# Earlier loads, another split of small steps, and weight maxima on ScalarE in the first stage of a two-layer cross-attention kernel

## The chip, the cores and the metric

The kernel runs on one core of one Trainium2 chip. The metric is the device time of one execution in microseconds (us), as the median of several runs. The engines are called PE (TensorE), DVE (VectorE), ACT (ScalarE), POOL (GpSimd) and SP (SyncE, which here issues transfers). A line number such as L986 is a line of the kernel before.

## The reference, cut to what matters

There are two layers over `x` of 4 x 1024 rows and 1024 columns. Layer 0 is a cross-attention that is one matrix product, layer 1 a softmax attention, and each is followed by a feed-forward part. The change touches only what must be done before the second half can start: the quantised product of layer 0, and the preparation of the weights of both feed-forward parts.

```python
def quant_dequant_act_1x128(x):            # x, after a layernorm: one scale per row and 128 columns
    amax = max(abs(xb)); safe = maximum(amax, 1e-4)
    return float8_e4m3(xb * (448 / safe)) * (safe / 448)
# the context: the same with one scale per block of 128 x 128
x = x + tanh(g_xattn[0]) * quant(layernorm(x)) @ quant(context).T
# the ternary feed-forward part
scale_x = max(abs(rms_norm(layernorm(x)) * gamma))        # one number over all rows
scale_w = mean(abs(weight)); w_q = round(clip(weight / scale_w, -1, 1))
x = x + tanh(g_ffn[0]) * (quantise8(...) @ w_q.T) * scale_w
# layer 1: softmax attention with the context as keys and values, then 8 experts (Wa, Wb), top 2
```

The one number `scale_x` needs all 32 row tiles of the first product, so the kernel has a stage 1 (this product, and the preparation of weights), then a short reduction, and then a stage 2 with all the rest.

## The kernel before, in words

Rows come in 32 tiles of 128, eight to a batch. Stage 1 is a software pipeline that is written out by hand on each engine as a loop over steps `j` from -11 to 33, and the order of the calls within a step is the order of the instructions on that engine. Engines meet only through semaphores. Step `j` works on several tiles at once.

A **row tile** `n` takes this way: SP loads it (`load_x`). DVE takes mean and variance (`x_stats`, L970 and L976), POOL the reciprocal root (`x_rstd`, L453 and L455), ACT subtracts the mean (`centre`, L620). DVE takes eight block maxima (`x_max`, L1004) and makes of them the scales in three small instructions of 8 columns (L1008, L1010, L1012). POOL makes the factors that undo the scale, as a high and a low part, in five small instructions (`x_factors`, L460 to L468). ACT scales (`x_scale`, L610), DVE prepares the rounding to eight bits in three wide instructions (`x_round_start`: L981 takes the exponent, L984 the step, L986 adds it), POOL subtracts it again (`x_round`, L482). ACT and POOL make the high and low half (`x_high`, L610; `x_low`, L475). SP transposes both, PE multiplies them with the context (L809), DVE adds the product to the row tile (`finish_x1`, L1070 and L1073), ACT squares it (`x1_square`, L653), and DVE takes a weighted maximum (`x1_max`, L1077). In step `j`, DVE does `x_max` of tile `j+3`, `x_stats` of `j+4`, `x1_max` of `j-2`, `x_round_start` of `j+2`, and `finish_x1` of `j-1`.

A **context tile** `m` is loaded by eight transfers of 64 KB (`load_c_rows`, L280). DVE takes its maximum (`c_max`, L1017). When all eight of a batch are in, `c_widest` and `c_factors` make the scales, with a transpose on PE between them (L785). Then ACT scales (L638), DVE prepares the rounding in the same three lines L981, L984 and L986 (`c_round_start`), POOL finishes it (`c_round`, L487), PE spreads it (`fill`, L797) and ACT writes the product's operands (`c_evict`, L647). The steps with `c_factors` are called table steps: -3, 5 and 13. One row of scratch for the rounding step serves the row tiles (XSTEP), another the context (CSTEP), so the next rounding waits until POOL has read the last.

**Weights.** From step 9 on, 24 pieces of the weights are loaded and DVE takes the sum or the maximum of each (`weight_stat`, L1082), two in a step. From step 24 on (`PREP`), eight rounds prepare three pieces each: ACT scales them (L658 to L660), DVE clips and rounds the ternary one (L1120, L1123) and takes the low halves of the others (L1128). The three raw pieces have one buffer each, so a round's loads wait for the round before (`load_prep`).

**The reduction.** When the last square is in, POOL takes two powers over all 32 columns (L531, L533), DVE and PE find the one maximum (L1177 to L1191), and the signal `go` (L1196) opens stage 2, whose first DVE instruction is L1201.

Of the kernel before, what the change touches and what calls it, by code (L numbers as in the profile page):

```python
# [5 lines left out]
P = 128  # L6
# [3 lines left out]
KB = D // P  # L10
# [22 lines left out]
TINY = 1e-30  # L33
# [12 lines left out]
STAT, PREP = 9, 24  # L46
# [4 lines left out]
W_TURN_AFTER = PREP - 3 + C_EVICT  # L51
FILL_HI, FILL_LO = 2.0 ** 6, 2.0 ** 14
# [13 lines left out]
def flamingo_two_layers(nc, x, ctx_in, g_xattn, g_ffn, w0, gamma, router_w, wa, wb, out):  # L66
    x_rows = x.rearrange("b s d -> (b s) d")
    c_rows = ctx_in.rearrange("b s d -> (b s) d")
    c_sets = ctx_in.rearrange("b (s r) (k q) -> b r s k q", s=GROUPS, k=KB)
# [6 lines left out]
    with ExitStack() as stack:  # L76
# [52 lines left out]
        W0, WA_RAW, WB_RAW = slot[11], slot[12], slot[3]  # L129
# [7 lines left out]
        CQ = lo_hi(rings[2][:, 3])  # L137
        w_hi = [wa_hi[:], arena[0][:].rearrange("p (k n) -> p k n", k=KB)]
# [4 lines left out]
        xd, xt1, xt2 = small(KB), small(KB), small(KB)  # L143
# [15 lines left out]
        ea, ec, ejunk, eab = (slot[6][:, i * TILES:(i + 1) * TILES] for i in range(4))  # L159
# [53 lines left out]
        c_in = signals("c_in", C_RING, 16 * CHUNK)  # L213
# [8 lines left out]
        x_d, x_hi, x_lo, x_turned = signal("x_d", 5), signal("x_hi"), signal("x_lo"), signals("x_turned", 2, 32)  # L222
# [39 lines left out]
        def weight_slot(t, kind):  # L262
            return t[:].rearrange("p (e r) -> p e r", e=E) if kind == 1 else t[:]
# [17 lines left out]

        @block.sync
        def _(sp):
            def load_c(m):
                after(sp, c_q, m - C_RING)
                for r in range(CHUNK):
                    load_c_rows(sp, m, r)

            for m in range(0, PER_BATCH, 2):
                load_c(m)  # L290
# [12 lines left out]
            def load_stat(t):  # L303
                kind, r = divmod(t, KB)
                after(sp, st_red, t - 2)
                sp.dma_start(weight_slot(WST[t % 2], kind), weight_tile(kind, r)).then_inc(st_in[t % 2].sem, 16)

            def load_prep(r):
                if r == 0:
                    sp.wait_ge(st_red.sem, st_red.at(3 * KB - 1))  # L310
                    sp.wait_ge(c_q.sem, c_q.at(TILES - 1))
                else:
                    sp.wait_ge(w_lo_set.sem, w_lo_set.at(r - 1))
                    sp.wait_ge(w_tern.sem, w_tern.at(r - 1))
                for kind, t in enumerate((W0, WA_RAW, WB_RAW)):
# [1058 lines left out]
```

## Time and profile before

| | us |
|---|---|
| median of 3 runs (2175.8 to 2178.02) | 2176.89 |
| the profiled execution, its own time | 2178.21 |
| its span, from the first to the last instruction | 2176.4 |
| busy in the span: PE, DVE, ACT, POOL | 1881.9, 1603.7, 1247.6, 909.7 |
| first product added (`finish_x1` of tile 0), last (tile 31) | 120.42, 567.43 |
| first DVE instruction of stage 2 | 585.15 |

The profile is of one execution. Busy is the time in which an engine had an instruction in flight. It includes time in which an instruction that had started was held up, so a busy engine need not be an engine at work: two instructions of the same shape with very different durations are the sign of it. The whole of what follows lies in the first 585 us.

### The profile page before, as it was taken

The numbers are of one execution on the slowest core, as the hardware profiler recorded it, in microseconds if no ns is written. First come the engines' busy times: TensorE is split into PE (matmuls) and PEld (weight loads), VectorE is DVE, ScalarE is ACT, GpSimd is POOL, SyncE is SP. The second block draws the span as 40 slices with busy tenths as digits, with TensorE's granted clock in tenths as the row PEclk, the third lists the DMA queues.
The fourth block names the chain that finished last, engine by engine and source line by source line (L and its number), as shares of the span: only waits on it lengthen the run. The fifth ranks groups of instructions, "written<-read, shape, count | busy, mean of one in ns | idle before, by whom it ended". The sixth has DMA issues, their size and how long they took to land.

```text
span 2176.4 us, 26455 instructions
## 1 busy us (share of the span) xinstructions
PE 1881.9 (86%) x8968; PEld 845.8 (39%) x8968; DVE 1603.7 (74%) x2297; ACT 1247.6 (57%) x2011; POOL 909.7 (42%) x1290
## 2 busy tenths in 40 slices
PE   1398768967548999999999999999999999999997
PEld 0144334423213444444444444444444444444443
DVE  5899989997356777777777777677777777777761
ACT  2677657765145556556565656556655656565650
POOL 2687868763223333333333333333333333333320
PEclk9999889988768999999999999999999999999998
DMA  5465656667447888887888787888888787878781
GB/s 142 137 158 149 196 144 188 165 184 203 131 89 141 167 162 162 159 163 153 169 158 172 159 170 151 160 168 165 157 160 165 153 166 161 170 159 170 129 151 43
DMA packets 924743, 339.97 MB, mean 156 GB/s; under 512 B 850753, under 2 KB 899905, under 8 KB 924609
## 3 DMA queue, kind: packets, MB, share of 16 engines
q1 hardware_dynamic: 920000, 336.19, 72.2%
q10 hardware_dynamic: 4608, 2.10, 0.4%
q8 instruction: 71, 1.16, 0.2%
q14 instruction: 64, 0.52, 0.1%
HBM read 92.83 MB, written 33.55 MB: 58 GB/s over the span
## 4 chain that ended last, share of the span: by engine, by line
DVE 35%; issue 18%; ACT 18%; PE 11%; POOL 9%; DMA 5%; SPq 4%; POOLq 0%; ACTq 0%; DVEq 0%
ACT slot L704 8%; DVE tiny L1227 7%; DVE tiny L970 5%; POOL tiny L567 5%; ACT arena L696 5%; POOL tiny L565 3%; PE sc L809 3%; DMA slot<-slot 3%; SPq L280 3%; DVE slot L1231 3%; ACT tiny L690 2%; DVE arena L1239 2%; DVE slot L1214 2%; DMA probs<-slot 2%; ACT slot L718 2%
## 5 line engine op out<-in xcount | busy, mean ns | idle before, releaser
L1231 DVE SCALAR_TENSOR_TENSOR slot<-arena,tiny,slot 128x1024 f16<-128x1024 f32 x256 | 328.4, 1283 | 313.7 <-ACT slot L704 313.7
L866 PE MATMUL sc<-arena,slot 128*128 128x512 f16 x1536 | 376.9, 386 | 34.6 <-ACT arena L696 24.9
L704 ACT ACTIVATE slot<-arena,tiny 128x1024 f16<-128x1024 f32 x256 | 293.7, 1147 | 178.3 <-POOL tiny L567 164.8
L565 POOL TENSOR_SCALAR tiny<-tiny 128x1 f32<-128x1 f32 x256 | 98.9, 386 | 698.1 <-ACT arena L696 698.1
L1227 DVE TENSOR_REDUCE tiny<-sc 128x1 f32<-128x1024 f32 x256 | 306.3, 1206 | 16.9 <-PE sc L866 16.5
L696 ACT ACTIVATE arena<-sc,tiny,head_tab 128x1024 f32<-128x1024 f32 x256 | 308.4, 1205 | 8.6
L690 ACT ACTIVATE tiny<-tiny,head_tab 128x1 f32<-128x1 f32 x256 | 73.9, 289 | 353.0 <-DVE tiny L1227 353.0
L809 PE MATMUL sc<-probs,slot 128*128 128x512 f16 x768 | 184.4, 404 | 66.1 <-DMA slot<-slot 65.5
L866 PEld LDWEIGHTS sc<-arena,slot 128*128 128x128 f16 x1536 | 151.2, 99 | 224.0 <-ACT arena L696 30.7
L882 PE MATMUL accs<-probs,arena 128*128 128x512 f16 x512 | 195.0, 381 | 13.8 <-issue 13.5
L849 PE MATMUL accs<-wb_hi,slot 128*128 128x512 f16 x512 | 195.1, 381 | 8.3 <-DMA slot<-slot 8.3
L851 PE MATMUL accs<-wa_hi,slot 128*128 128x512 f16 x512 | 196.8, 384 | 0.0
L850 PE MATMUL accs<-wa_lo,slot 128*128 128x512 f16 x512 | 196.5, 384 | 0.0
L849 PE MATMUL accs<-wa_hi,slot 128*128 128x512 f16 x512 | 196.2, 383 | 0.0
L883 PE MATMUL accs<-probs,arena 128*128 128x512 f16 x512 | 195.2, 381 | 0.0
L884 PE MATMUL accs<-probs,arena 128*128 128x512 f16 x512 | 195.1, 381 | 0.0
L850 PE MATMUL accs<-wb_lo,slot 128*128 128x512 f16 x512 | 195.1, 381 | 0.0
L851 PE MATMUL accs<-wb_hi,slot 128*128 128x512 f16 x512 | 195.0, 381 | 0.0
L567 POOL TENSOR_TENSOR tiny<-tiny,neg_one 128x1 f32<-128x1 f32 x256 | 160.1, 625 | 21.3
L809 PE MATMUL sc<-wa_hi,slot 128*128 128x512 f16 x512 | 139.5, 390 | 25.7 <-DMA slot<-slot 18.0
L809 PEld LDWEIGHTS sc<-probs,slot 128*128 128x128 f16 x768 | 77.7, 103 | 171.0 <-DMA slot<-slot 70.9
L551 POOL TENSOR_TENSOR slot<-slot 128x512 f16<-128x512 f32 x64 | 74.1, 1158 | 146.0 <-ACT slot L733 146.0
(195 smaller groups left out, 3183.2 us busy)
## 6 DMA issues: line engine op xcount, KB each, us to landing
arena<-in_x SPq DMA_DIRECT2D x32, 512.0 KB, 3.5
x_scratch<-arena SPq DMA_DIRECT2D x32, 512.0 KB, 3.0
slot<-x_scratch SPq DMA_DIRECT2D x32, 512.0 KB, 4.0
slot<-in_ctx SPq DMA_DIRECT2D x32, 512.0 KB, 4.3
out<-arena SPq DMA_DIRECT2D x32, 512.0 KB, 3.4
slot<-in_L_ffn_weight SPq DMA_DIRECT2D x16, 512.0 KB, 3.9
slot<-in_L_ffn_Wa SPq DMA_DIRECT2D x16, 512.0 KB, 5.0
slot<-in_L_ffn_Wb SPq DMA_DIRECT2D x16, 512.0 KB, 5.5
```

The costliest lines, as they stand in the source:

```text
L567: pool.tensor_tensor(rinv[c % 2][:], rsum[c % 2][:], neg_one[:], ALU.pow).then_inc(s_ri.sem, 1)
L696: act.activation(PF[c % 2], sc[:, c % 2, :], ACT.Exp, bias=nbias[c % 2][:], scale=head_tab[:, n, 1:2], accum_out=rsum[c % 2][:]).then_inc( ...
L704: act.activation(PH[c % 2], PF[c % 2], ACT.Identity, scale=rinv[c % 2][:]).then_inc(s_ph.sem, 1)
L809: mm = pe.matmul(sc[:, j % 2, h * HALF:(h + 1) * HALF], lhs[:, cols], rhs[:, k, h * HALF:(h + 1) * HALF], start=start, stop=stop)
L849: pe.matmul(accs[:, a, :], lhs_hi, r_hi[:, k, cols], start=k == 0, stop=False)
L850: pe.matmul(accs[:, a, :], lhs_hi, r_lo[:, k, cols], start=False, stop=False)
L851: mm = pe.matmul(accs[:, a, :], lhs_lo, r_hi[:, k, cols], start=False, stop=k == KB - 1)
L866: mm = pe.matmul(sc[:, c % 2, h * HALF:(h + 1) * HALF], q[i][:, c * P:(c + 1) * P], k[j][:, h * HALF:(h + 1) * HALF], start=start, stop=stop)
L883: pe.matmul(accs[:, ACC_V, :], v[0][:, cols], PT[:, h, KB + j, :], start=False, stop=False)
L884: mm = pe.matmul(accs[:, ACC_V, :], v[1][:, cols], PT[:, h, j, :], start=False, stop=j == KB - 1)
L1227: dve.tensor_reduce(nmx[c % 2][:], sc[:, c % 2, :], AX.X, ALU.max, negate=True).then_inc(s_mx.sem, 1)
L1231: dve.scalar_tensor_tensor(out=PL[c % 2], in0=PF[c % 2], scalar=rinv[c % 2][:], in1=PH[c % 2], op0=ALU.mult, op1=ALU.subtract).then_inc(s_ ...
```

## The change

It has these parts.

- **Loads.** The context of the first batch and three tiles more come in three groups (4, 4 and 3 tiles), each as eight transfers over all tiles of the group, one for each block of 128 columns and 16 partitions wide (`load_c_columns`), four from SP and four from ACT. Tiles 11 to 14 come in two pairs in the same way. The first two row tiles are loaded ahead of them, and their whole preparation stands ahead of the loop on all engines, between the context's first maxima.
- **Small steps.** L1008 and L1012 become instructions with two tensor inputs (the constant lies in a small tile of 8 columns). The five instructions of `x_factors` on POOL become three on DVE, two-input ones too, right behind `x_max`.
- **Weight maxima.** `weight_stat` moves from DVE to ACT, as an absolute value or a square with a sum, about one a step from step 0 to 20, and POOL takes two roots afterwards.
- **Weight preparation.** The raw pieces get a second set of buffers, `load_prep` runs up to two rounds ahead, and on ACT `weight_high` stands behind `x1_square`, not ahead of it.
- **Reduction.** POOL's powers are taken four columns at a time from step 24 on, so that the last four are left for the end.
- `round_start` is split into `round_step` and `round_add`, which are called one after the other.

The order on POOL in a step of the kernel before with a row tile and a context tile (`x_rstd`, `x_factors`, `x_round`, `c_round`, `x_low`):

```order
L453 TENSOR_SCALAR tiny<-xmv 128x1 [waits x_st]
L455 TENSOR_TENSOR tiny<-tiny,neg_half 128x1 [waits x_ra]
L460 TENSOR_SCALAR tiny<-xsafe 128x8 [waits x_am]
L462 TENSOR_SCALAR tiny<-tiny 128x8 [waits x_d]
L464 TENSOR_TENSOR tiny<-tiny 128x8 [waits x_d]
L466 TENSOR_TENSOR slot<-tiny 128x8 [waits x_d]
L468 TENSOR_TENSOR slot<-tiny,slot 128x8 [waits x_d]
L482 TENSOR_TENSOR slot<-slot,arena 128x1024 [waits x_u]
L487 TENSOR_TENSOR wb_lo<-wb_lo,slot 128x1024 [waits c_fill,c_u]
L475 TENSOR_TENSOR slot<-slot 128x1024 [waits x_d,x_q]
```

The same step in the changed kernel (L514 and L516 are `x_rstd`, L530 is `x_round`, L535 `c_round`, L523 `x_low`):

```order
L514 TENSOR_SCALAR tiny<-xmv 128x1 [waits x_rs,x_st]
L516 TENSOR_TENSOR tiny<-tiny,neg_half 128x1 [waits x_ra]
L530 TENSOR_TENSOR slot<-slot,arena 128x1024 [waits x_lo,x_hi,x_u]
L535 TENSOR_TENSOR wb_lo<-tern,slot 128x1024 [waits c_fill,c_u]
L523 TENSOR_TENSOR slot<-slot 128x1024 [waits x_turned0,x_d,x_q]
```

The five small instructions are gone, and `x_rstd` stands right ahead of `x_round`.

On DVE, `x_max` and what follows it up to the statistics of the next tile, before:

```order
L1004 TENSOR_REDUCE tiny<-slot 128x8 [waits x_xc]
L1008 TENSOR_SCALAR xsafe<-tiny 128x8 [waits x_rs,x_am]
L1010 RECIPROCAL tiny<-xsafe 128x8 [waits x_am]
L1012 TENSOR_SCALAR xk<-tiny 128x8 [waits x_am]
L970 BN_STATS tiny<-arena 128x6 [waits x_in1]
```

And in the changed kernel:

```order
L1092 TENSOR_REDUCE tiny<-slot 128x8 [waits x_d,x_k,x_xc]
L1096 SCALAR_TENSOR_TENSOR xsafe<-tiny 128x8 [waits x_rs,x_am]
L1099 RECIPROCAL tiny<-xsafe 128x8 [waits x_am]
L1101 SCALAR_TENSOR_TENSOR xk<-tiny 128x8 [waits x_am]
L1107 SCALAR_TENSOR_TENSOR tiny<-xsafe 128x8
L1110 SCALAR_TENSOR_TENSOR slot<-xsafe,tiny 128x8 [waits x_d]
L1113 TENSOR_TENSOR slot<-xsafe,slot 128x8 [waits x_d]
L1051 BN_STATS tiny<-arena 128x6 [waits x_st,x_in1]
```

Five instructions of 8 columns with two tensor inputs and one reciprocal stand there now, where there were two with one input and the reciprocal.

On ACT, a step of the weight preparation before (L610 is `x_high` and then `x_scale`, L620 `centre`, L658 to L660 `weight_high`, L653 `x1_square`):

```order
L610 ACTIVATE slot<-slot 128x128 x8
L610 ACTIVATE slot<-slot,xk 128x128 x8
L620 ACTIVATE slot<-arena,xmv 128x1024
L658 ACTIVATE slot<-slot,tiny 128x1024
L659 ACTIVATE wa_hi<-slot,tiny 128x1024
L660 ACTIVATE wb_hi<-slot,tiny 128x1024
L653 ACTIVATE slot,row_tab<-arena,row_tab 128x1024
```

And in the changed kernel (L714 is `x1_square`, L721 to L723 `weight_high`):

```order
L671 ACTIVATE slot<-slot 128x128 x8
L671 ACTIVATE slot<-slot,xk 128x128 x8
L681 ACTIVATE slot<-arena,xmv 128x1024
L714 ACTIVATE slot,row_tab<-arena,row_tab 128x1024
L721 ACTIVATE slot<-slot,tiny 128x1024
L722 ACTIVATE wa_hi<-slot,tiny 128x1024
L723 ACTIVATE wb_hi<-slot,tiny 128x1024
```

The square, which waits for the step's `finish_x1` on DVE, has moved ahead of the three weight instructions.

The diff, cut to its core:

```diff
+STAT_STEPS = 21
+C_GROUPS = ((0, 4), (4, 4), (8, 3))
+C_PAIRS = {11: 2, 12: 0, 13: 2, 14: 0}
+X_EARLY, NORM_COLS = 2, 4
+PREP_TILES = (25, 26, 27)
...
+        RAW_EARLY = [rings[1][:, 2], rings[1][:, 3], rings[2][:, 2]]
+        RAW_LATE = [XP[tile % X_RING] for tile in PREP_TILES]
+        def raw(kind, r):
+            if r % 2 == 0:
+                return RAW[kind]
+            return (RAW_EARLY if r < KB // 2 else RAW_LATE)[kind]
...
+        def load_c_columns(eng, m, count, k, sig):
+            b, i = divmod(m, PER_BATCH)
+            at = m % C_RING
+            ring = (tern, wb_hi, wb_lo)[at // 4][:].rearrange("p e n -> p (e n)").bitcast(F32)
+            dst = ring[k::KB, (at % 4) * D:(at % 4 + count) * D].rearrange("p (r q) -> p r q", q=P)
+            src = c_columns[b, k][:, i * CHUNK:(i + count) * CHUNK]
+            eng.dma_start(dst, src).then_inc(sig.sem, 16)
...
             def load_prep(r):
-                if r == 0:
+                if r < 2:
...
-                    sp.wait_ge(w_lo_set.sem, w_lo_set.at(r - 1))
-                    sp.wait_ge(w_tern.sem, w_tern.at(r - 1))
+                    sp.wait_ge(w_lo_set.sem, w_lo_set.at(r - 2))
+                    sp.wait_ge(w_tern.sem, w_tern.at(r - 2))
+                if r == KB // 2 + 1:
+                    sp.wait_ge(x1_out.sem, x1_out.at(PREP_TILES[-1]))
+                    sp.wait_ge(e_sq.sem, e_sq.at(PREP_TILES[-1]))
...
+                for r in range(KB):
+                    late = 1 if r % 2 and r > KB // 2 else 2
+                    if j == PREP - late + r:
+                        load_prep(r)
...
-            def x_factors(n):
-                pool.wait_ge(x_am.sem, x_am.at(n, 2))
-                pool.tensor_scalar(xd[:], xsafe[:, n % 2], -AMP / FP8_MAX, 1.0, ALU.mult, ALU.mult).then_inc(x_d.sem, 1)
...
+            def row_norms(first, count):
+                cols = slice(first, first + count)
+                pool.wait_ge(e_sq.sem, e_sq.at(first + count - 1))
+                pool.tensor_scalar(ea[:, cols], row_tab[:, cols, 1], ...)
+                pool.tensor_tensor(ec[:, cols], ea[:, cols], neg_half[:, cols], ALU.pow).then_inc(g_pool.sem, 1)
+                pool.wait_ge(e_max.sem, e_max.at(first + count - 1))
+                pool.tensor_tensor(eab[:, cols], row_ab[:, cols], half_pow[:, cols], ALU.pow).then_inc(g_pool.sem, 1)
...
         @block.scalar
-            for m in range(1, PER_BATCH, 2):
-                for r in range(CHUNK):
-                    load_c_rows(act, m, r)
-            act.wait_ge(const_in.sem, 48)
+            for g, (first, count) in enumerate(C_GROUPS):
+                for k in range(KB // 2, KB):
+                    load_c_columns(act, first, count, k, c0_in[g])
...
+            def weight_stat(t):
+                act.wait_ge(st_in[t % 2].sem, st_in[t % 2].at(t // 2))
+                act.activation(WST[t % 2][:], WST[t % 2][:], ACT.Abs if t < KB else ACT.Square,
+                               accum_out=wst[:, t:t + 1]).then_inc(st_red.sem, 1)
+            for n in range(X_EARLY):
+                centre(n)
+            for n in range(X_EARLY):
+                x_scale(n)
+            for n in range(X_EARLY):
+                x_high(n)
...
+                if is_x(j - 1):
+                    x1_square(j - 1)
+                for t in stats_of(j):
+                    weight_stat(t)
                 if PREP <= j < PREP + KB:
                     weight_high(j - PREP)
-                if is_x(j - 1):
-                    x1_square(j - 1)
...
         @block.vector
-                dve.tensor_scalar(xsafe[:, i], xam[:], xrstd[:, i:i + 1], ACT_EPS, ALU.mult, ALU.max).then_inc(x_am.sem, 1)
+                dve.scalar_tensor_tensor(out=xsafe[:, i], in0=xam[:], scalar=xrstd[:, i:i + 1], in1=eps8, op0=ALU.mult,
+                                         op1=ALU.max).then_inc(x_am.sem, 1)
...
+            def x_factors(n):
+                d, hi, lo = xsafe[:, n % 2], xdh[:, n % 4], xdl[:, n % 4]
+                dve.scalar_tensor_tensor(out=xt2[:], in0=d, scalar=SPLIT7, in1=d, op0=ALU.mult, op1=ALU.subtract)
+                dve.scalar_tensor_tensor(out=hi, in0=d, scalar=SPLIT7, in1=xt2[:], op0=ALU.mult, op1=ALU.subtract)
+                dve.tensor_tensor(lo, d, hi, ALU.subtract).then_inc(x_d.sem, 1)
...
-            for m in range(PER_BATCH):
+            for n in range(X_EARLY):
+                x_stats(n)
+            for n in range(X_EARLY):
+                x_max(n)
+            for m in range(PER_BATCH // 2):
+                c_max(m)
+            for n in range(X_EARLY):
+                x_round_start(n)
+            for m in range(PER_BATCH // 2, PER_BATCH):
                 c_max(m)
...
-                if STAT <= j < STAT + 12:
-                    weight_stat(2 * (j - STAT))
-                    weight_stat(2 * (j - STAT) + 1)
```

## Rows read from the trace of the kernel before

**Rows 1.** Stretches: busy us of each engine and count, granted clock, transfer share, GB/s
```profile
120.42:415.82 295.40, 242.66 (x1131) 112.47 (x1129) 279.41 (x437) 197.94 (x441) 230.32 (x209) 0.93 0.62 170
...
567.43:585.23 17.80, 0.63 (x2) 0.25 (x2) 4.42 (x16) 1.24 (x2) 12.11 (x3) 0.59 0.38 147
```

**Rows 2.** Timeline of DVE, `finish_x1`: start us, duration us, engine, line
```profile
120.42 1.28 DVE L1070 SCALAR_TENSOR_TENSOR arena<-sc,tiny,arena 128x1024 f32<-128x1024 f32 x1
...
161.20 1.28 DVE L1070 SCALAR_TENSOR_TENSOR arena<-sc,tiny,arena 128x1024 f32<-128x1024 f32 x1
...
180.31 1.28 DVE L1070 SCALAR_TENSOR_TENSOR arena<-sc,tiny,arena 128x1024 f32<-128x1024 f32 x1
...
192.09 1.28 DVE L1070 SCALAR_TENSOR_TENSOR arena<-sc,tiny,arena 128x1024 f32<-128x1024 f32 x1
...
275.10 1.28 DVE L1070 SCALAR_TENSOR_TENSOR arena<-sc,tiny,arena 128x1024 f32<-128x1024 f32 x1
...
304.45 1.28 DVE L1070 SCALAR_TENSOR_TENSOR arena<-sc,tiny,arena 128x1024 f32<-128x1024 f32 x1
...
415.82 1.28 DVE L1070 SCALAR_TENSOR_TENSOR arena<-sc,tiny,arena 128x1024 f32<-128x1024 f32 x1
...
449.65 1.28 DVE L1070 SCALAR_TENSOR_TENSOR arena<-sc,tiny,arena 128x1024 f32<-128x1024 f32 x1
...
567.43 1.28 DVE L1070 SCALAR_TENSOR_TENSOR arena<-sc,tiny,arena 128x1024 f32<-128x1024 f32 x1 [5.15 <-PE sc L809]
```

**Rows 3.** Timeline of POOL and DVE around table step 5
```profile
175.91 2.21 POOL L482 TENSOR_TENSOR slot<-slot,arena 128x1024 f16<-128x1024 f32 x1
176.17 2.50 DVE L981 TENSOR_SCALAR slot<-wb_hi 128x1024 uint16<-128x1024 uint16 x1
...
182.56 1.90 POOL L475 TENSOR_TENSOR slot<-slot 128x1024 f16<-128x1024 f16 x1
...
184.07 0.41 DVE L1008 TENSOR_SCALAR xsafe<-tiny 128x8 f32<-128x8 f32 x1
```

**Rows 4.** Timeline of POOL and DVE in step 24
```profile
453.10 1.90 POOL L475 TENSOR_TENSOR slot<-slot 128x1024 f16<-128x1024 f16 x1
453.10 1.97 DVE L1115 SCALAR_TENSOR_TENSOR rw_hl<-slot,tiny,rw_hl 128x64 f16<-128x64 f32 x1
```

**Rows 5.** Groups: form xcount | busy us, mean ns | idle before
```profile
L1271 DVE SCALAR_TENSOR_TENSOR tiny<-tiny 128x8 f32<-128x8 f32 x32 | 7.3, 229 | 1.1
...
L653 ACT ACTIVATE slot<-arena,row_tab 128x1024 f32<-128x1024 f32 x32 | 36.6, 1144 | 66.5 <-DVE row_tab L1073 66.3
```

**Rows 6.** Timeline of the start
```profile
0.73 10.39 ACTq L280 DMA_DIRECT2D tern<-in_ctx  x16
...
21.55 1.28 ACT L605 ACT_TABLE_LOAD   x1 [21.55 <-issue]
...
23.74 2.34 DVE L1017 TENSOR_REDUCE slot<-wb_hi 128x1 f32<-128x1024 f32 x2 [2.46 <-DMA wb_hi<-in_ctx]
...
26.20 0.16 DVE L1022 TENSOR_REDUCE tiny<-slot 128x1 f32<-128x8 f32 x1
...
31.99 0.69 DVE L981 TENSOR_SCALAR slot<-tern 128x1024 uint16<-128x1024 uint16 x1
```

**Rows 7.** Timeline, one context rounding ahead of the first row tile
```profile
47.22 0.68 DVE L981 TENSOR_SCALAR slot<-tern 128x1024 uint16<-128x1024 uint16 x1
...
49.70 2.12 POOL L487 TENSOR_TENSOR wb_lo<-tern,slot 128x1024 f16<-128x1024 f32 x1 [3.03 <-DVE tern L986]
```

**Rows 8.** SP's issue of two Wa pieces (each of 1024 runs of 512 bytes)
```profile
280.95 1.50 SPq L306 DMA_DIRECT2D slot<-in_L_ffn_Wa  x2
```

**Rows 9.** Waits of DVE in stage 1: us in total, times, longest
```profile
DVE slot L1031 <- PE accs L785: 8.9, 2, 8.3
```

**Rows 10.** Chain of waits, weight preparation: start us, us, what
```profile
474.94 6.58 DMA slot<-in_L_ffn_Wb
```

**Rows 11.** Timeline, the first DVE instruction of stage 2
```profile
585.15 1.28 DVE L1201 SCALAR_TENSOR_TENSOR slot<-slot,row_tab,gamma_b 128x1024 f32<-128x1024 f32 x1
```

More of the change, by code:

```diff
@@ L158, in flamingo_two_layers @@
             small(), small())
-        ea, ec, ejunk, eab = (slot[6][:, i * TILES:(i + 1) * TILES] for i in range(4))
+        ea, ec, ejunk, eab = (small(TILES) for i in range(4))
         esum = small(2)
@@ L271, in is_x, with maxima_of, stats_of @@
             return 0 <= n < TILES
+        def maxima_of(j):
+            return [m for m in range(PER_BATCH, TILES)
+                    if j == (min(m - C_MAX + 1, -4) if m < 2 * PER_BATCH else m - C_MAX)]
+        def stats_of(j):
+            return [t for t in range(3 * KB) if t * STAT_STEPS // (3 * KB) == j]
         def is_c(m, start=0):
@@ L280, in load_c_rows, with c_loaded @@
             eng.dma_start(C[m % C_RING][:, r * P:(r + 1) * P], c_sets[b, i * CHUNK + r]).then_inc(ring.sem, 16)
+        def load_c_columns(eng, m, count, k, sig):
[5 more added lines that the diff above has]
+            eng.dma_start(dst, src).then_inc(sig.sem, 16)
+        def c_loaded(eng, m):
+            for g, (first, count) in enumerate(C_GROUPS):
+                if first <= m < first + count:
+                    eng.wait_ge(c0_in[g].sem, c0_in[g].at(0))
+                    return
+            if C_PAIRS.get(m, 1) == 0:
+                m -= 1
+            earlier = [k for k in range(C_RING, m) if k % C_RING == m % C_RING and C_PAIRS.get(k, 1)]
+            eng.wait_ge(c_in[m % C_RING].sem, c_in[m % C_RING].at(len(earlier)))
         @block.sync
@@ L284, in load_c @@
             def load_c(m):
-                after(sp, c_q, m - C_RING)
-                for r in range(CHUNK):
-                    load_c_rows(sp, m, r)
-            for m in range(0, PER_BATCH, 2):
-                load_c(m)
+                count = C_PAIRS.get(m, 1)
+                if count == 0:
+                    return
+                after(sp, c_q, m + count - 1 - C_RING)
+                if count == 2:
+                    for k in range(KB):
+                        load_c_columns(sp, m, count, k, c_in[m % C_RING])
+                else:
+                    for r in range(CHUNK):
+                        load_c_rows(sp, m, r)
+            for n in range(X_EARLY):
+                sp.dma_start(XP[n], rows(x_rows, n)).then_inc(x_in[n].sem, 16)
+            for g, (first, count) in enumerate(C_GROUPS):
+                for k in range(KB // 2):
+                    load_c_columns(sp, first, count, k, c0_in[g])
             sp.dma_start(gate_in[:, 0:2], g_xattn.partition_broadcast(P)).then_inc(const_in.sem, 16)
@@ L600, in _ @@
         def _(act):
-            for m in range(1, PER_BATCH, 2):
-                for r in range(CHUNK):
-                    load_c_rows(act, m, r)
-            act.wait_ge(const_in.sem, 48)
-            act.activation(gate[:], gate_in[:], ACT.Tanh).then_inc(gates.sem, 1)
-            act.activation(GSQ[:], gamma_b[:], ACT.Square).then_inc(gsq.sem, 1)
+            for g, (first, count) in enumerate(C_GROUPS):
+                for k in range(KB // 2, KB):
+                    load_c_columns(act, first, count, k, c0_in[g])
             def by_block(dst, src, factors, sig):
```

172 lines of the change are left out of this document (97 added, 75 removed).

## The prediction, made before the changed kernel was run

> **What bounds the kernel now.** I read the stretches first, then DVE's timeline at every `finish_x1`, then POOL beside DVE, then the waits, and last the end of stage 1. The change lies ahead of `go`, so I follow the first 585 us alone and leave the rest, up to 2176.4, as it is. The stretches show DVE busy for 279.41 of 295.40 us while the row tiles pass, with ACT at 197.94 and POOL at 230.32 [rows 1]: DVE sets the pace, and work that goes to ACT has cover there. The clock was 0.93 with PE busy for 242.66 [rows 1], which is not the bound.
>
> DVE's busy time holds some that is no work. L981, 0.69 when alone [rows 6], took 2.50 when POOL's L482 was running as it started; L1008, eight columns, took 0.41 while POOL's L475 ended [rows 3]. A wide POOL instruction and some DVE instructions hold each other up. The cost of a step is therefore what DVE issues and which POOL instruction starts inside it.
>
> The yardstick is the start of each `finish_x1` [rows 2]. It cuts the time into: start to tile 0, 120.42; tiles 0 to 20, 295.40, of which a plain step is 11.78 at its shortest (180.31 to 192.09), the table steps 19.11 (161.20 to 180.31) and 29.35 (275.10 to 304.45), and so the other 18 steps 246.94, or 13.72 each; tiles 20 to 23, 33.83; tiles 23 to 31 (weight preparation), 117.78, or 14.72 a step; and from there to stage 2, 17.72 [rows 2, 11].
>
> **1. Loads and the start.** An issue of a context transfer costs 10.39 / 16 = 0.65 [rows 6]. In the changed kernel ACT issues 12 first: 0.73 + 7.8 = 8.5; a table load (1.28 [rows 6]) and one pass of `centre` (1.14, the mean of L653 [rows 5]) end at 10.9. The row tiles' statistics lie beside that. Then DVE has, ahead of the first context rounding: two row tiles of a maximum 1.17 (L1017 has the same size [rows 6]), six small instructions of 0.23 (L1271's shape [rows 5]) and a rounding of 2.48 (L981 to the start of POOL's L487, 47.22 to 49.70 [rows 7]), 10.1 together; eight context maxima, 8 x 1.17 = 9.4; waits for POOL between the two tiles, one rounding 2.12 [rows 7] and one `x_low` 1.90 [rows 3], 4.0; and the tables, which took 26.20 to 31.99 [rows 6], or 4.6 less one maximum that is counted already. Sum 39.0 where it was 31.99: 7.0 later.
>
> From there to tile 0 it was 120.42 - 31.99 = 88.4. The two row tiles' 10.1 leaves this stretch. Six context steps were bound by eight issues, 8 x 0.65 = 5.2; with two to four tiles in the same issues they are bound by DVE and POOL, since the next rounding waits until POOL has read CSTEP: 2.48 + 2.12 = 4.6 [rows 7], and 6 x 0.6 = 3.6 goes. The three steps with row tiles get three small instructions more, 3 x 0.7 = +2.1. So 76.8, tile 0 at 115.8: **-4.6**. Bounds: what the column transfers cost to issue is not shown. The nearest row has 0.75 for a piece of 1024 runs [rows 8]; that is near 0.65, which I keep. The other end is a price by runs, as in rival B. Below, -9: if the waits for POOL at the start vanish.
>
> **2. The plain steps.** DVE loses nothing there but two of its weight maxima a step from 9 on, and gains three small instructions, 3 x 0.23 = 0.7 [rows 5]. POOL loses the five small ones ahead of `x_round`, so `x_round` starts as soon as DVE has finished the row tile's L986. That is the moment at which DVE goes on to the context's rounding. It lets POOL in between L981 and L984 and has to wait, which I price by the one case shown: 2.50 - 0.69 = 1.81 [rows 3, 6]. A step is then 11.78 + 0.7 + 1.8 = 14.3 against the mean of 13.72, in which such delays stand already, at other places. 18 x (14.3 - 13.72) = +10.4. Bounds: 0 for the delay, 18 x (12.5 - 13.72) = -22; and the delay on top of the old ones, rival C.
>
> A rule of the Trainium skill speaks against the new small steps ("SBUF — State Buffer", section "Who interferes with whom"): a DVE instruction with two SBUF inputs uses the port pair that it shares with GpSimd, and whoever starts first keeps it to the end. By it five small instructions could each wait for a whole POOL instruction; this trace agrees in one place, where L1115, 64 columns and two SBUF inputs, started with POOL's L475 at 453.10 and took 1.97 against its 1.90 [rows 4]. I charge one such wait of a wide POOL instruction a step, and it is in 11.78 already, in the 0.41 of L1008 [rows 3]; without any, rival A.
>
> **3. Table steps.** Of the second, 29.35, DVE waited 8.3 for the transpose on PE [rows 9], behind loads and turns that the weight maxima had pushed back. Two maxima a step become one, in other buffers of the order, and ACT has 97 us free in that stretch [rows 1]; I let it fall to the first one's 19.1: 29.35 - 19.1 = **-10.2**. It may keep half of that, -5. Together with the plain steps: 18 x 14.3 + 2 x 19.1 = 295.6, no change.
>
> **4. Tiles 20 to 23.** Nothing heavy enters or leaves: 33.83 stays, give or take 3.
>
> **5. Weight preparation.** The context is over, so a step's row work on DVE is 11.78 - 2.48 - 1.17 + 0.7 = 8.8. `weight_high` now stands behind the square, and the square behind the step's `finish_x1`. DVE, which clips, rounds and takes low halves, waits for 1.28 [rows 2], a square 1.14, three ACT passes 3.4 [rows 5], and has then two wide passes of some 1.17 for the last piece, 8.2 in all, where one pass of 1.14 was seen of it before: +7.0. Four steps with a whole row tile are 15.9 each. The last four have less and less row work; their lower end is the round trip and its `x1_max`, 9.7, the upper one the full step; 12.2 is nearer to the lower, as most of the row work is gone. 4 x 15.9 + 4 x 12.2 = 112.4 against 117.78: **-5.4**. What pays for the longer round trip is the second set of raw buffers: a Wb piece was 6.58 from issue to landing on the chain [rows 10], and a load up to two rounds ahead takes it off. If none of that is gained, +4 x 1.2 = +5; if the trip is hidden too, -20.
>
> **6. The reduction.** POOL's three instructions over 32 columns took 12.11 of the 17.80 at the end [rows 1]. Four columns by the column are 1.5, -10.6; three instructions as long as any wide one here (2.2 [rows 3]) would be 6.6, -5.5. I take **-10**, near the column price: an average of 4.0 for 32 columns, where a plain instruction takes 2.2 for 1024, says that it is the powers' elements that cost. Behind it come `x1_max` and DVE's own 4.42, not shortened.
>
> **Sum**: -4.6 (start) + 10.4 - 10.2 (tiles 0 to 20) + 0 - 5.4 - 10 = -19.8. On the profiled execution's span, 2156.6; on its own time, 2178.21 - 19.8 = 2158.4; that execution lies 1.3 above the median of the runs, so the median becomes **2157**. The likeliest case by itself is 2145 to 2168.
>
> **Rivals.**
> A. The small instructions never wait for POOL: eight columns with two inputs slip in, as L1271 does at 229 ns [rows 5], and the delay of the context's rounding falls to 1 us: about 18 x 0.8 = 14 less. For it: POOL is free for long parts of a step. Against it: L1115 [rows 4]. 2143.
> B. The column transfers cost by the run: 16 partitions with many short runs each. If each of the 12 issues took four times as long, 2.6 us, ACT would be free 12 x 1.95 = 23 later and tile 0 with it. Against it: 0.75 for 1024 runs [rows 8]. 2180, no change.
> C. Slower. `x_round`, now unhindered, collides with the context's rounding on top of the delays that were there, not in place of them: a plain step is 13.72 + 0.7 + 1.81 = 16.2, and 18 x 2.5 = +45 stands against the other terms, -4.6 - 10.2 - 5.4 - 10 = -30.2: +15, 2192. It decides from 30.2 / 18 = 1.7 a step, that is from steps of 15.4. For it: POOL's 230.32 of 295.40 [rows 1] leave few gaps in which a wide instruction starts unnoticed. Against it: POOL has five instructions less, so its wide ones have more room.
>
> **Chances.** Forecast 0.64, A 0.14, B 0.08, C 0.12, and 0.02 for weight preparation gaining all of its 20. Two runs of this kernel are told apart at about 0.2%, 4.4 us. Faster holds the forecast without its slow edge (0.62), A and the last, 0.78; no change holds that edge and B, 0.10; slower is C, 0.12. The range goes down past A and the bounds of terms 1 and 5 to 2136, and up nearly to B, 2177; C and half of B lie above it, some 0.03 below.
>
> **What would show it.** The first `finish_x1` starts near 116, the tile-23 one near 445. A plain step is 14.3 and the context's step (L984 before) is longer there by 1.8 than where no POOL instruction runs; under A the step is 13.5, under C over 15.4. The second table step is near 19; were it still 29, the transposes are held by something else. A step of the weight preparation is near 16 with ACT's `weight_high` behind DVE on the chain of waits. From the last `finish_x1` to stage 2 it is under 9. B shows at once, in the time of ACT's first 12 issues: 7.8 or over 30. Most of all the forecast is wrong if tiles 0 to 20 take other than 290 to 301 us, since that is 20 steps times an unproven collision.

## The result

| | before | changed | predicted |
|---|---|---|---|
| median of 5 runs each, us | 2176.89 | 2162.01 (2161.12 to 2164.91) | 2157 (2136 to 2177) |
| ratio to before | | 0.9926, 95% interval 0.9909 to 0.9942 | 0.991 |
| profiled execution: own time, span | 2178.21, 2176.4 | 2161.88, 2159.8 | span 2156.6 |
| POOL busy, DVE busy in the span | 909.7, 1603.7 | 836.2, 1601.8 | |

The change makes the kernel faster by 0.6 to 0.9%. In the profile the span is 16.6 us shorter; 19.8 was predicted. By the prediction's own stretches (the changed kernel's `finish_x1` is L1171, its `go` is followed by L1303):

| stretch | before | predicted | changed | difference, predicted and measured |
|---|---|---|---|---|
| start to tile 0 | 120.42 | 115.8 | 122.02 | -4.6, **+1.6** |
| tiles 0 to 20 | 295.40 | 295.6 | 293.03 | +0.2, -2.4 |
| of it a plain step / second table step | 13.72 mean / 29.35 | 14.3 / 19.1 | 14.07, mean 14.19 / 18.87 | |
| tiles 20 to 23 | 33.83 | 33.8 | 32.70 | 0, -1.1 |
| tiles 23 to 31 | 117.78 | 112.4 | 110.72 | -5.4, -7.1 |
| tile 31 to stage 2 | 17.72 | 7.7 | 8.83 | -10, -8.9 |
| stage 2 | 1591.3 | 1591.3 | 1592.5 | 0, +1.2 |

Stage 2 is the same code. Between the twelve profiled executions of this case it took 1591.3 to 1595.2 us, so its 1.2 is noise, and a difference of a few us in a total is to be read from the stretches. Means are over the 18 steps that are not table steps.

### The profile page after: what moved, and what is told of

Same layout as the page of the kernel before. It is cut to its first block, busy times and chain, and to the rows that moved or that the text cites. A ratio compares the mean times of both kernels' runs of the same rounds, so it can differ in the third digit from the quotient of the medians.

```text
span 2159.8 us, 26457 instructions
## 1 busy us (share of the span) xinstructions
PE 1881.5 (87%) x8968; PEld 846.1 (39%) x8968; DVE 1601.8 (74%) x2369; ACT 1273.0 (59%) x2059; POOL 836.2 (39%) x1154
## 4 chain that ended last, share of the span: by engine, by line
DVE 35%; issue 20%; ACT 18%; PE 12%; POOL 9%; DMA 4%; SPq 0%; POOLq 0%; ACTq 0%; DVEq 0%
ACT slot L784 8%; DVE tiny L1329 7%; DVE tiny L1051 5%; POOL tiny L631 5%; ACT arena L776 4%; POOL tiny L629 3%; ACT tiny L770 2%; DVE slot L1333 2%; DMA slot<-slot 2%; PE sc L889 2%; DVE slot L1065 2%; DVE arena L1341 2%; DVE slot L1316 2%; PE sc L947 2%; DMA probs<-slot 2%
## 5 line engine op out<-in xcount | busy, mean ns | idle before, releaser
L889 PE MATMUL sc<-probs,slot 128*128 128x512 f16 x768 | 179.2, 396 | 47.7 <-DMA slot<-slot 44.1
L889 PEld LDWEIGHTS sc<-probs,slot 128*128 128x128 f16 x768 | 76.8, 101 | 147.7 <-DMA slot<-slot 48.2
```

The lines of the kernel that those rows point to most:

```text
L889: mm = pe.matmul(sc[:, j % 2, h * HALF:(h + 1) * HALF], lhs[:, cols], rhs[:, k, h * HALF:(h + 1) * HALF], start=start, stop=stop)
```

## The profile after

DVE's timeline at `finish_x1` of the changed kernel, against [rows 2]; the columns are as there:

```profile
122.02 1.28 DVE L1171 SCALAR_TENSOR_TENSOR arena<-sc,tiny,arena 128x1024 f32<-128x1024 f32 x1
...
182.96 1.28 DVE L1171 SCALAR_TENSOR_TENSOR arena<-sc,tiny,arena 128x1024 f32<-128x1024 f32 x1
...
197.03 1.28 DVE L1171 SCALAR_TENSOR_TENSOR arena<-sc,tiny,arena 128x1024 f32<-128x1024 f32 x1
...
281.83 1.28 DVE L1171 SCALAR_TENSOR_TENSOR arena<-sc,tiny,arena 128x1024 f32<-128x1024 f32 x1
...
300.70 1.28 DVE L1171 SCALAR_TENSOR_TENSOR arena<-sc,tiny,arena 128x1024 f32<-128x1024 f32 x1
```

182.96 to 197.03 is a plain step, 281.83 to 300.70 the second table step. The stretches (as in [rows 1]) show that POOL lost work and DVE did not become less busy:

```profile
122.02:415.05 293.03, 238.99 (x1105) 110.47 (x1106) 281.45 (x474) 218.73 (x483) 172.50 (x109) 0.92 0.58 163
447.75:558.47 110.72, 83.61 (x350) 35.33 (x348) 81.78 (x127) 61.96 (x123) 48.75 (x39) 0.89 0.71 185
558.47:567.30 8.83, 0.64 (x2) 0.26 (x2) 4.34 (x16) 1.24 (x2) 3.21 (x3) 0.62 0.56 204
```

POOL went from 230.32 to 172.50 in the first stretch, DVE from 279.41 to 281.45. The reason stands in one plain step, DVE first and POOL under it:

```profile
219.43 0.43 DVE L1065 TENSOR_SCALAR arena<-arena 128x1024 bf16<-128x1024 bf16 x1
219.89 1.22 DVE L1069 TENSOR_TENSOR slot<-slot,arena 128x1024 f32<-128x1024 f32 x1
221.03 0.69 DVE L1062 TENSOR_SCALAR slot<-wb_hi 128x1024 uint16<-128x1024 uint16 x1
221.75 2.23 DVE L1065 TENSOR_SCALAR slot<-slot 128x1024 bf16<-128x1024 bf16 x1
```
```profile
221.19 2.51 POOL L530 TENSOR_TENSOR slot<-slot,arena 128x1024 f16<-128x1024 f32 x1 [1.30 <-DVE slot L1069]
```

L1065 stands there twice with one shape: 0.43 for the row tile, 2.23 for the context, because POOL's `x_round` (L530) started as the row tile's L1069 ended, and L1065 ends 0.28 behind it (223.98 and 223.70). This is the collision of the prediction, 1.80 where it had 1.81. The kernel before was held for as long in a plain step ahead of its weight maxima, at two small instructions that take 0.23 each when free:

```profile
137.78 0.88 DVE L1008 TENSOR_SCALAR xsafe<-tiny 128x8 f32<-128x8 f32 x1
...
138.93 1.58 DVE L1012 TENSOR_SCALAR xk<-tiny 128x8 f32<-128x8 f32 x1
```

That is 0.65 and 1.35, 2.00 together, against 1.80 and the 0.18 by which L1096 is held in the changed kernel (0.41). What makes the step longer, 14.07 for 13.58, are the three small instructions: from L1101's start to that of the next wide instruction it is 0.62, where it was 0.14 from L1012's when nothing held it. From step 9 on the kernel before took 14.09: two weight maxima stood there, 2.33 in all, and the hold was 0.24. So there the maxima that went to ACT gave DVE nothing, since the hold came back and the small instructions were added.

At the start, ACT's queue, against [rows 6]:

```profile
0.73 2.92 ACTq L312 DMA_DIRECT2D tern<-in_ctx  x4
3.68 6.96 ACTq L312 DMA_DIRECT2D wb_hi<-in_ctx  x4
10.66 6.10 ACTq L312 DMA_DIRECT2D wb_lo<-in_ctx  x4
```

The first four issues cost 0.73 each, the next 1.74, the last 1.52: 15.98 for twelve, where the prediction had 7.8. And at the end POOL's three instructions, 12.11 before [rows 1]:

```profile
561.31 1.23 POOL L555 TENSOR_SCALAR tiny<-row_tab 128x4 f32<-128x4 f32 x1 [26.77 <-ACT slot L714]
562.62 1.01 POOL L558 TENSOR_TENSOR tiny<-tiny,neg_half 128x4 f32<-128x4 f32 x1
563.60 1.01 POOL L560 TENSOR_TENSOR tiny<-row_ab,half_pow 128x4 f32<-128x4 f32 x1
```

In the weight preparation, one full step of the changed kernel, ACT and then DVE:

```profile
465.69 1.15 ACT L714 ACTIVATE slot<-arena,row_tab 128x1024 f32<-128x1024 f32 x1 [3.25 <-DVE row_tab L1174]
...
466.84 1.13 ACT L721 ACTIVATE wb_hi<-wb_hi,tiny 128x1024 f32<-128x1024 f32 x1
```
```profile
465.50 0.15 DVE L1174 TENSOR_SCALAR row_tab<-tiny 128x1 f32<-128x1 f32 x1
468.00 0.69 DVE L1217 TENSOR_SCALAR wb_hi<-wb_hi 128x1024 f32<-128x1024 f32 x1 [2.35 <-ACT wb_hi L721]
```

ACT waits 3.25 for DVE's L1174, then DVE waits 2.35 for ACT's square and first weight piece: the round trip that the prediction charged.

## The experiments

All start from the changed kernel and are timed beside the kernel before on the same chip. Line numbers in a profile are that kernel's own; the names in the text hold.

**e1, the start.** ACT's third group is issued later:

```diff
-            for g, (first, count) in enumerate(C_GROUPS):
+            for g, (first, count) in enumerate(C_GROUPS[:2]):
...
                 x_scale(n)
+            for k in range(KB // 2, KB):
+                load_c_columns(act, C_GROUPS[2][0], C_GROUPS[2][1], k, c0_in[2])
```

> The changed kernel, with ACT's four transfers of the third context group issued behind x_scale of the first two row tiles, not ahead of centre. Theory A (the step of the prediction that failed is the price of an issue: ACT's 12 issues took 15.98 us, not 7.8, and centre started at 16.85): the first centre starts near 11, the first context rounding near 41 instead of 46.4, the first finish_x1 near 116 to 117 instead of 122.0, median near 2157. Rival B (the context's own arrival sets the first rounding): centre starts early, but the second group of maxima waits for its data, the first rounding stays within 1.5 us of 46.4 and the median within 2 us of 2162.

Measured: 2158.36 us, ratio 0.9899 (0.988 to 0.9918). ACT's queue and DVE at tile 0:

```profile
3.72 7.82 ACTq L312 DMA_DIRECT2D wb_hi<-in_ctx  x4
...
18.75 0.56 ACTq L312 DMA_DIRECT2D wb_lo<-in_ctx  x1
19.35 0.64 ACTq L312 DMA_DIRECT2D wb_lo<-in_ctx  x1
```
```profile
41.21 0.69 DVE L1064 TENSOR_SCALAR slot<-tern 128x1024 uint16<-128x1024 uint16 x1
...
116.94 1.28 DVE L1173 SCALAR_TENSOR_TENSOR arena<-sc,tiny,arena 128x1024 f32<-128x1024 f32 x1
```

The first context rounding in the changed kernel:

```profile
46.42 0.69 DVE L1062 TENSOR_SCALAR slot<-tern 128x1024 uint16<-128x1024 uint16 x1
```

Theory A: the first context rounding is at 41.21 instead of 46.42, tile 0 at 116.94 instead of 122.02, which is 3.5 below the kernel before. The same third group costs 0.56 to 0.64 an issue eight us later, so its 1.52 is no price of its transfers: it depends on when they are issued. That the loads in flight held the queue is my reading; the runs show only that the same issue is dear early and cheap late. The number of issues alone does not do it: in the kernel before, ACT issued sixteen at 0.65 ([rows 6]) while SP issued sixteen in 10.69 us, of 64 KB each, where these are of 192 and 256 KB.

**e2, the collision.** DVE's `x_stats` and `x1_max` go between the two roundings, POOL's `x_rstd` and `c_tables` behind `x_round`:

```diff
-                if is_x(j + 4) and j + 4 >= X_EARLY:
-                    x_stats(j + 4)
-                if is_x(j - 2):
-                    x1_max(j - 2)
...
                     x_round_start(j + 2)
+                if is_x(j + 4) and j + 4 >= X_EARLY:
+                    x_stats(j + 4)
+                if is_x(j - 2):
+                    x1_max(j - 2)
```

> The changed kernel, with DVE's order in a step turned: x_stats and x1_max stand between the row tile's rounding and the context's, and POOL's x_rstd behind x_round. Theory A (a plain step is 14.07 because the context's L1065 is held for 1.8 us by POOL's x_round, which now starts under it): L1065 of the context falls from 2.23 to 0.43, a plain step from 14.07 to 12.3 to 12.8, tiles 0 to 20 from 293.0 to 265 to 272 us, median near 2138. Rival B (the held-up time moves to another instruction of DVE, such as x1_max with its two SBUF inputs, or the transposes and PE are late next): a plain step stays above 13.5 and the median above 2152.

Measured: 2149.97 us, ratio 0.9861 (0.9838 to 0.9885); a plain step 13.02, tiles 0 to 20 276.1. DVE in a plain step, POOL's L530 there, and `x1_max` (L1178) in the changed kernel:

```profile
212.23 1.94 DVE L1178 CUSTOM_DVE_ANT_0 slot<-slot 128x1024 f32<-128x1024 f32 x1
214.10 0.08 DVE L1178 DVE_READ_ACCUMULATOR2_ANT row_ab<- 128x1 f32 x1
214.10 0.68 DVE L1062 TENSOR_SCALAR slot<-wb_hi 128x1024 uint16<-128x1024 uint16 x1
214.81 0.43 DVE L1065 TENSOR_SCALAR slot<-slot 128x1024 bf16<-128x1024 bf16 x1
```
```profile
210.95 2.13 POOL L530 TENSOR_TENSOR slot<-slot,arena 128x1024 f16<-128x1024 f32 x1 [3.41 <-DVE slot L1069]
```
```profile
217.60 1.17 DVE L1178 CUSTOM_DVE_ANT_0 slot<-slot 128x1024 f32<-128x1024 f32 x1
```

Between the two: the context's L1065 is 0.43, as theory A has it, and the step loses 1.05, not the 1.3 to 1.8 that A asked for, since `x1_max`, 1.17 before, is now 1.94 (0.77 go back, as rival B said of it). Tiles 20 to 23 took 37.2 instead of 32.7: there DVE waited 5.2 for PE (L1201), where it had waited 0.8.

**e3, the small instructions on POOL again,** as five, and the call on DVE behind `x_max` taken out, with the waits that go with them:

```diff
+                pool.tensor_scalar(xd[:], xsafe[:, n % 2], -AMP / FP8_MAX, 1.0, ALU.mult, ALU.mult).then_inc(x_d.sem, 1)
...
+                pool.tensor_tensor(xdl[:, n % 4], xd[:], xdh[:, n % 4], ALU.subtract).then_inc(x_d.sem, 1)
...
-                x_factors(n)
```

> The changed kernel, with x_factors as five small instructions on POOL again, as in the kernel before; all other parts stay. Theory A (the move to DVE made plain steps longer, 13.58 to 14.07, since it freed x_round to start under the context's rounding): a plain step goes back to 13.6, the context's L1065 to 0.43, tiles 0 to 20 to about 285 us, median near 2154, faster than the changed kernel by 6 to 9 us. Rival B (the move is a gain, and other parts made the steps longer): a plain step goes to 14.3 or more, median 2165 or more.

Measured: 2154.93 us, ratio 0.9888 (0.9867 to 0.9908); a plain step 13.59, tiles 0 to 20 280.7, tile 0 at 117.09. POOL ahead of `x_round` (L543), and DVE's small ones and the context's rounding (L1082):

```profile
212.51 1.19 POOL L521 TENSOR_SCALAR tiny<-xsafe 128x8 f32<-128x8 f32 x1
...
214.86 1.18 POOL L527 TENSOR_TENSOR slot<-tiny 128x8 f32<-128x8 f32 x1
216.12 0.20 POOL L529 TENSOR_TENSOR slot<-tiny,slot 128x8 f32<-128x8 f32 x1
216.28 2.13 POOL L543 TENSOR_TENSOR slot<-slot,arena 128x1024 f16<-128x1024 f32 x1
```
```profile
206.07 0.87 DVE L1113 SCALAR_TENSOR_TENSOR xsafe<-tiny 128x8 f32<-128x8 f32 x1
...
207.21 1.58 DVE L1118 SCALAR_TENSOR_TENSOR xk<-tiny 128x8 f32<-128x8 f32 x1
...
214.29 0.43 DVE L1082 TENSOR_SCALAR slot<-slot 128x1024 bf16<-128x1024 bf16 x1
```

Theory A's numbers hold, its reason does not. Tiles 0 to 20 fall by 12.4: 16 plain steps give 9.0, two steps of 11.8 behind the table steps 4.9, and the table steps take 1.6 back. Tile 0 gains 4.9. Tiles 20 to 31 give 6.4 back (149.8 instead of 143.4). The five small instructions on POOL are a delay of 3.8 us that keeps `x_round` off the context's rounding, which is 0.43 again. But what is held up instead costs the same: L1113 and L1118 take 0.64 and 1.35 longer than their 0.23, 1.99 together, for 1.98 in the changed kernel. The 0.48 that a plain step gains are the three small instructions that DVE no longer issues. So this part of the change is a loss by itself, by its work on DVE and not by the place of the collision; only in the two steps of 11.8 is the hold shorter, by 1.8.

**e4, the weight preparation.** `weight_high` ahead of `x1_square` again, the early loads kept:

```diff
+                if PREP <= j < PREP + KB:
+                    weight_high(j - PREP)
                 if is_x(j - 1):
                     x1_square(j - 1)
...
-                if PREP <= j < PREP + KB:
-                    weight_high(j - PREP)
```

> The changed kernel, with ACT's weight_high ahead of x1_square again; the second set of raw buffers and the early loads stay. Theory A (in the weight preparation the loads gave all the gain, and the new place of weight_high costs DVE a wait for the square in each step): a full step falls from 16.4 to about 15.3, tiles 23 to 31 from 110.7 to 100 to 104 us, median near 2154. Rival B (the raw pieces still come late, so that ACT would stand at them with the square behind): a step stays at 16 or more, tiles 23 to 31 at 110 or more, median 2162 or more.

Measured: 2150.9 us, ratio 0.9874 (0.9849 to 0.9898); a full step 13.50, tiles 23 to 31 97.67. In the step, and ACT's wait for raw pieces from tile 23 to 31 (total, times, longest), in the kernel before and then in e4:

```profile
463.25 0.15 DVE L1174 TENSOR_SCALAR row_tab<-tiny 128x1 f32<-128x1 f32 x1
463.32 1.45 DVE L1217 TENSOR_SCALAR wb_hi<-wb_hi 128x1024 f32<-128x1024 f32 x1
```
```profile
ACT slot L658 <- DMA slot<-in_L_ffn_Wb: 33.6, 7, 8.8
```
```profile
ACT arena L721 <- DMA arena<-in_L_ffn_Wb: 19.5, 2, 9.8
```

Theory A, beyond its numbers. DVE goes from L1174 to L1217 without a wait. The new place of the weights on ACT therefore cost 13 us. Tiles 23 to 31 took 117.78 before with this order, so all other parts together are worth about 20 there. That this is mostly the loads and their second buffers is likely, since ACT waited for a raw piece in seven rounds before and in two here, but no run takes the loads away alone.

**e5 and e6, the second table step.** e5 keeps the maxima on ACT in the old schedule; e6 keeps the new schedule and puts them on DVE, as a sum or a maximum again, so that POOL's two roots become a multiplication by one:

```diff
-            return [t for t in range(3 * KB) if t * STAT_STEPS // (3 * KB) == j]
+            return [2 * (j - 9), 2 * (j - 9) + 1] if 9 <= j < 21 else []
```
```diff
+                dve.tensor_reduce(wst[:, t:t + 1], WST[t % 2][:], AX.X, ALU.add if t < KB else ALU.max,
+                                  apply_absolute_value=True).then_inc(st_red.sem, 1)
```

> The changed kernel, with the weight maxima in the schedule of the kernel before, two a step from step 9 to 20, but still on ACT. Theory A (in the kernel before the second table step took 29.35 us since the second load of a step stands on SP ahead of the transposes and waits for the maxima of the last step, two a step being the cause): the second table step (tile 11 to 12) goes from 18.87 to 27 to 30, median near 2171. Rival B (the engine is the cause: DVE, held in c_factors, was late with its maxima, ACT is not): the second table step stays at 18 to 20, median within 2 us of 2162.

> The changed kernel, with the weight maxima on DVE again, in the schedule of the changed kernel, about one a step from step 0 to 20. Theory A (the schedule took the 10 us off the second table step, and ACT only hides the maxima themselves): each of the 24 maxima costs DVE 1.2 us, the plain steps go from 14.07 to about 15.2, the second table step stays at 19 to 21, tiles 0 to 20 take about 318 us, median near 2187. Rival B (the engine is the cause): the second table step goes to 27 or more, median 2193 or more. Rival C (POOL's work gives the maxima cover, and they fall in time in which DVE was held): plain steps stay below 14.5, median below 2172.

Measured, e5: 2180.08 us, ratio 1.0006 (0.999 to 1.0022); second table step 26.31. e6: 2176.91 us, ratio 0.9988 (0.9974 to 1.0001); second table step 20.00, plain steps 15.01 up to tile 12 and 14.07 from tile 14 on. SP around the table step, the changed kernel and then e5:

```profile
277.73 4.35 SPq L378 DMA_TRANSPOSE slot<-slot  x2
```
```profile
285.85 1.42 SPq L358 DMA_DIRECT2D slot<-in_L_ffn_Wa  x2
287.38 4.13 SPq L378 DMA_TRANSPOSE slot<-slot  x2
```

The schedule is most of it (7.4 of 10.5): with two maxima a step, SP stands at two loads until the last maxima are done (L358 waited up to 2.5 for ACT's L727), and the transposes that PE needs come 10 us later behind them; DVE's wait for PE's transpose in e5 (total, times, longest) is near the 8.3 of [rows 9]:

```profile
DVE slot L1132 <- PE accs L865: 7.3, 1, 7.3
```

The 3.0 between 26.31 and 29.35 stay open. In kernels with the same code around it this step varies by up to 2 (18.87 in the changed kernel and 19.16 in e4, 22.18 in e8 and 20.39 in e10), so a difference of that size is not read. e5 lost more than this step: some steps from 16 on and tiles 20 to 23 too. In e6 theory A holds for the table step and for the first half; from tile 14 on, where no context maximum stands in the step any more, a maximum on DVE costs nothing, because it fills time in which L1096 is held in the changed kernel (first line; 0.41 in e6, second line). So tiles 0 to 20 took 305.0, not the 318 of A.

```profile
345.93 1.49 DVE L1096 SCALAR_TENSOR_TENSOR xsafe<-tiny 128x8 f32<-128x8 f32 x1
```
```profile
361.05 0.41 DVE L1094 SCALAR_TENSOR_TENSOR xsafe<-tiny 128x8 f32<-128x8 f32 x1
```

**e7, two inputs or one.** L1096 and L1101 as `tensor_scalar`, as before:

```diff
-                dve.scalar_tensor_tensor(out=xsafe[:, i], in0=xam[:], scalar=xrstd[:, i:i + 1], in1=eps8, op0=ALU.mult,
-                                         op1=ALU.max).then_inc(x_am.sem, 1)
+                dve.tensor_scalar(xsafe[:, i], xam[:], xrstd[:, i:i + 1], ACT_EPS, ALU.mult, ALU.max).then_inc(x_am.sem, 1)
```

> The changed kernel, with L1096 and L1101 as instructions with one tensor input and a constant, as in the kernel before. Theory A (a small instruction of DVE that starts beside a wide one of POOL waits for its end in either form, so this part of the change is worth nothing): L1096 stays at 0.41 us in a plain step, the step at 14.07, median within 2 us of 2162. Rival B (the one-input form is held up more often, as L1008 and L1012 were in the kernel before with 0.87 and 1.58): a plain step is 14.5 or more and the median 2169 or more.

Measured: 2163.62 us, ratio 0.9928 (0.9904 to 0.9952), a plain step 14.07. The line in this kernel and in the changed one (smallest, median, largest ns):

```profile
L1096 DVE TENSOR_SCALAR xsafe<-tiny x32: 231/408/1802, 20.8 to 510.4; 128x8 f32<-128x8 f32 x32
```
```profile
L1096 DVE SCALAR_TENSOR_TENSOR xsafe<-tiny x32: 226/407/1801, 20.6 to 507.5; 128x8 f32<-128x8 f32 x32
```

Theory A: the two forms are held alike, to 1 ns in the median. This part is worth nothing.

**e8, e10, e9, what the runs point to.** e8 has the edits of e1, e2 and e4. e10 has e2's order only ahead of step 24. e9 has e10's and this on PE:

```diff
+                if j in TABLE_STEPS:
+                    c_spread_max((j + 11) // PER_BATCH)
                 if is_x(j):
...
                     product(j, range(KB // 2))
-                if j in TABLE_STEPS:
-                    c_spread_max((j + 11) // PER_BATCH)
```

> Three of the edits together: ACT's third context group behind x_scale, x_stats and x1_max between the two roundings, weight_high ahead of x1_square. Theory A (the three act in different stretches and add up): tile 0 near 115.5, tiles 0 to 20 in 276, tiles 20 to 23 in 37, tiles 23 to 31 in 98, median near 2131, below both kernels. Rival B (an earlier start or the shorter steps meet loads that come no earlier, and a part of the gain is lost): median 2138 or more.

> The three edits together, with the new order of x_stats and x1_max only ahead of step 24 and the old one in the weight preparation, where no context rounding follows the row tile's. Theory A (in the weight preparation the new order only puts x1_max beside POOL's x_round): a full step there falls from 14.8 to 13.5 as with weight_high alone, tiles 23 to 31 from 102.8 to 98, median near 2128. Rival B (the shorter time is taken back by transposes and loads that come no earlier): tiles 23 to 31 stay above 101, median within 2 us of 2133.

> The kernel with the order by stage, and on PE the transpose for the context's tables ahead of the step's product, not in the middle of it. Theory A (what is left of the second table step, 22.18 with the three edits, is DVE's wait of 4.4 us for that transpose behind a product whose row tile is turned late): both table steps fall, the second to 16 to 18, median 4 to 6 us below the order by stage alone. Rival B (the transpose waits for ACT's eviction of the context tile before, so that the product behind it is late and finish_x1 waits for that instead): the table steps stay or grow, median not below.

| | median | ratio to before | tile 0 | 0 to 20 | second table step | 20 to 23 | 23 to 31 |
|---|---|---|---|---|---|---|---|
| changed | 2162.01 | 0.9926 (0.9909 to 0.9942) | 122.02 | 293.0 | 18.87 | 32.7 | 110.7 |
| e8 | 2133.11 | 0.979 (0.9765 to 0.9814) | 114.10 | 277.3 | 22.18 | 35.5 | 102.8 |
| e10 | 2129.32 | 0.9769 (0.9756 to 0.9783) | 114.12 | 276.0 | 20.39 | 36.4 | 97.7 |
| e9 | 2126.40 | 0.9756 (0.9743 to 0.9769) | 114.13 | 273.5 | 17.69 | 36.1 | 96.9 |

The three edits add up (A; 2131 expected). e10 confirms A: in the weight preparation the new order had cost 5 us. In e9 the second table step falls to 17.69, inside A's 16 to 18, and DVE's wait for the transpose (4.4 in e8, 2.6 in e10) is gone; the first stays at 17.69, where A had both falling; its median is 2.9 below e10's, less than the 4 to 6 expected, and the two intervals overlap, so of the total only the sign is likely. e9 is below both kernels, by 2.4% and 1.6%.

## Why the prediction was right, and where it was not

- **Start: the step that failed.** "An issue of a context transfer costs 0.65" was nearly true of the first five (0.64 to 0.78) and of the third group when it came late (e1), not of the seven between, which took 1.27 to 2.65. Twelve cost 15.98 instead of 7.8, and that 8.2 is more than the whole miss of 6.2 at tile 0. The rest of the term held: from the first context rounding to tile 0 75.6, predicted 76.8. Rival B had the direction, not the mechanism: it priced by runs, and all groups of one size would have cost the same. The first two groups are of one size and took 2.92 and 6.96.
- **Plain steps.** Right in mechanism and nearly in size: 14.07, or 14.19 in the mean, for 14.3. The added small instructions are 0.16 to 0.17 each, not 0.23; the hold is 1.80. e2 takes it away, less what `x1_max` pays, and e3 moves it back to two small instructions at the same size.
- **Table steps.** 18.87 for 19.1; so near is luck, as the step varies by up to 2 in like kernels. The cause was SP, as the prediction read it from [rows 9]; e5 shows it is the schedule and not the engine that the change's words name.
- **Weight preparation.** 110.7 for 112.4, a full step 16.42 for 15.9. e4 shows what the sum hid: +13 from the order and -20 from everything else, most of it probably the loads. The prediction had the -20 as a bound ("if the trip is hidden too, -20"). Its lower end for the last four steps, 9.7, adds up to 9.4 from the terms given.
- **Reduction.** -8.9 for -10. POOL did not go down to a price by the column: about 1 us for a power of four columns, between the two bounds given. The average of 4.0 that spoke for the column price mixed a multiplication of 1.25 with two powers of 5.45.
- **Rivals.** A is out: L1065 is held for the full 1.80 and L1096 for part of an instruction. C is out: a plain step is 0.35 above the old mean (0.47 mean against mean), not 2.5, since the old delays went with the five instructions on POOL (e3 brings both back).
- **The total** is nearer than its terms. The start was 6.2 too low and the end with stage 2 2.3, and the three stretches between were 5.4 too high, so that some 3 us are left. That they cancel is luck.

The Trainium skill's rule that was weighed ("SBUF — State Buffer", section "Who interferes with whom") said that a DVE instruction with two inputs in SBUF contends with a GpSimd instruction that reads SBUF. Two traces agree: L1225 in the changed kernel, next, with POOL's `x_low` under it, and `x1_max` in e2. The longest hold of a plain step is no case of this rule, since L1065 has one tensor input.

```profile
470.08 2.17 DVE L1225 SCALAR_TENSOR_TENSOR wa_lo<-wb_hi,tiny,wa_hi 128x1024 f16<-128x1024 f32 x1 [0.66 <-ACT wb_hi L723]
472.18 1.27 DVE L1225 SCALAR_TENSOR_TENSOR wb_lo<-wb_lo,tiny,wb_hi 128x1024 f16<-128x1024 f32 x1
```
```profile
468.79 2.39 POOL L523 TENSOR_TENSOR slot<-slot 128x1024 f16<-128x1024 f16 x1
```

The first of two equal ones took 0.9 longer while POOL's `x_low` ran (468.79 to 471.18).

## What to carry to other kernels

Work that goes from an engine that is not the bottleneck to the one that is costs its own time there, and it need not shorten the waits between the two: with the five small instructions gone from POOL, DVE was held at the context's rounding and not at two small instructions, for the same 2.0 us a step, and the three new instructions were 0.48 on top. So look for the same line with two durations and ask what will start under it after the change; then put instructions that are not held (here statistics) into that stretch. A change of many parts should be undone part by part: of the parts here, two were losses, worth 7 and 11 us by the medians of e3 and e4, which the net gain of 15 hid.

## What the runs showed that was not expected

- An issue of the same kind of transfer took 0.6 us or up to 2.65 us; for the third group (1.52 early, 0.56 to 0.64 late) it went by when it was issued; ACT's first work, the table load for `centre`, started at 16.85, right behind its last issue.
- A two-input instruction of 8 columns and a one-input one were held alike, 407 and 408 ns in the median (e7).
- POOL's instructions of 8 columns took 0.20 to 1.19 us in one step of e3, the long ones beside wide DVE instructions: the hold goes both ways.
- A hold on DVE moved with the order of instructions and kept its size: in the plain steps up to tile 8 it is 2.00 us before, 1.98 in the changed kernel, 1.99 in e3.
